# Two GIN layers on one core: all strided copies of layer 2 stored behind the dense stage, and 110 rows of edges summed from natural tiles first

## What is computed

```python
def _gin_conv(x, src, dst, n, W1, b1, gamma, beta, W2, b2):
    agg = jax.ops.segment_sum(x[src], dst, num_segments=n)
    h = x + agg
    h = jax.nn.relu(_batchnorm(h @ W1 + b1, gamma, beta))
    return jax.nn.relu(h @ W2 + b2)

h = jnp.maximum(_layernorm(x, axis=-1), 0.0)
h = _batchnorm(h, g0, b0)
h = jax.nn.relu(_gin_conv(h, src, dst, n, W1a, b1a, g1, bt1, W1b, b1b))
h = _gin_conv(h, src, dst, n, W2a, b2a, g2, bt2, W2b, b2b)
return x + jax.nn.relu(h)
```

## Time and profile before

| | us |
|---|---|
| median of 3 runs (2820.1 to 2820.8) | 2820.61 |
| the profiled execution | 2806.54 |
| its span, from the first to the last instruction | 2804.7 |
| PE busy | 2380.3 (85%) |
| POOL busy | 1846.7 (66%) |
| DVE busy | 1734.9 (62%) |
| ACT busy | 528.8 (19%) |
| DMA, mean rate over the span | 262 GB/s |

### The profile page before, as it was taken

How to read it: one execution, slowest core, us unless ns; L and a number is a source line. 1 busy time by engine, 2 the same in 40 slices (tenths; PEclk the granted TensorE clock), 3 DMA queues, 4 the chain that set the end, 5 groups by cost and what they waited for, 6 DMA issues and landing times.

```text
span 2804.7 us, 30481 instructions
## 1 busy us (share of the span) xinstructions
PE 2380.3 (85%) x10221; PEld 1829.1 (65%) x10221; DVE 1734.9 (62%) x3349; ACT 528.8 (19%) x1542; POOL 1846.7 (66%) x1870
## 2 busy tenths in 40 slices
PE   1466657999999999999998666799999999989879
PEld 1133424788777777777776544588888888776767
DVE  6999995655555555555556577655555555544459
ACT  8963534300000000000007611100000000000038
POOL 2058886777777777777770277777777777777720
PEclk8685766999999999999998899999999999999999
DMA  9387994888888888888874999988888888888868
GB/s 307 144 263 203 300 311 123 254 267 254 254 254 254 254 254 253 254 254 254 253 242 161 338 354 353 301 282 288 284 284 287 284 283 287 259 254 254 253 204 271
DMA packets 309073, 735.46 MB, mean 262 GB/s; under 512 B 41126, under 2 KB 183346, under 8 KB 308910
## 3 DMA queue, kind: packets, MB, share of 16 engines
q0 software_dynamic: 148896, 552.17, 62.7%
q1 hardware_dynamic: 160014, 181.25, 20.0%
HBM read 580.67 MB, written 152.59 MB: 261 GB/s over the span
## 4 chain that ended last, share of the span: by engine, by line
PE 49%; DMA 21%; POOL 13%; SPq 7%; issue 5%; ACT 5%; DVE 1%; DVEq 0%; ACTq 0%; POOLq 0%
PE agg_ps L815 33%; DMA rows<-node_rows,src_all 19%; POOL rows L687 8%; SPq L610 7%; PE mm_ps L940 6%; PE mm_ps L857 5%; POOL rows L672 3%; PE mm_ps L861 2%; POOL raw_more L672 2%; ACT acc L985 2%; ACT lane_code L972 1%; PE agg_ps L769 1%; ACT lane_code L961 1%; DMA raw_more<-node_rows,src_all 1%; DMA node_rows<-acc 1%
## 5 line engine op out<-in xcount | busy, mean ns | idle before, releaser
L687 POOL DMA_INDIRECT rows<-node_rows,src_all x1672 | 1580.4, 945 | 647.6 <-issue 347.9
L815 PE MATMUL agg_ps<-rows,work 128*128 128x256 f32 (+1 forms) x7106 | 1662.4, 387 | 179.7 <-DMA rows<-node_rows,src_all 136.0
L815 PEld LDWEIGHTS agg_ps<-rows,work 128*128 128x128 f32 x7106 | 1311.0, 190 | 502.9 <-DMA rows<-node_rows,src_all 122.9
L1514 DVE SCALAR_TENSOR_TENSOR acc<-agg_ps,in_first,acc 128x256 f32 (+1 forms) x289 | 140.0, 485 | 955.9 <-PE agg_ps L815 880.7
L1016 ACT ACTIVATE bn_root<-bn_var 128x2 f32<-128x2 f32 x3 | 0.6, 204 | 1891.1 <-DVE bn_var L1146 1891.1
L672 POOL DMA_INDIRECT rows<-node_rows,src_all x96 | 137.2, 1429 | 166.2 <-DMA node_rows<-acc 137.2
L1466 DVE TENSOR_TENSOR work<-lane_code,lane_ps 128x1024 f32<-128x1024 f32 (+1 forms) x209 | 231.6, 1108 | 1.1 <-issue 1.1
L940 PE MATMUL mm_ps<-early,work 128*128 128x256 f32 x784 | 176.1, 389 | 20.0 <-ACT work L1095 11.4
L940 PEld LDWEIGHTS mm_ps<-early,work 128*128 128x128 f32 x784 | 141.0, 194 | 55.3 <-issue 23.4
L1475 DVE TENSOR_TENSOR work<-lane_code,lane_ps 128x640 f32<-128x640 f32 x209 | 169.8, 812 | 0.0
L1095 ACT ACTIVATE work<-acc,bn_shift,bn_scale 128x128 f32<-128x128 f32 x392 | 167.3, 485 | 3.3 <-DVE bn_shift L1157 2.8
(11 more groups left out here) (250 smaller groups left out, 1663.7 us busy)
## 6 DMA issues: line engine op xcount, KB each, us to landing
node_rows<-acc SPq DMA_DIRECT2D x113, 260.0 KB, 5.7
rows<-node_rows,src_all POOLq DMA_INDIRECT x1768, 4.3
node_rows<-acc SPq DMA_DIRECT2D x27, 910.0 KB, 4.3
node_rows<-acc SPq DMA_DIRECT2D x57, 390.0 KB, 5.9
node_rows<-acc SPq DMA_DIRECT2D x28, 650.0 KB, 7.7
node_rows<-acc SPq DMA_DIRECT2D x114, 130.0 KB, 4.6
acc<-in_x SPq DMA_DIRECT2D x13, 896.0 KB, 11.0
rows<-in_x SPq DMA_DIRECT2D x13, 896.0 KB, 7.4
```

Of the source, the lines that this page charges most:

```text
L687: pool.indirect_dma_start(tile_rows(k, 0, ROWS_OF[t] * DP), None, tables[layer][0:NPOS if t >= LAST_STRIDED else TABLE, :], bass.IndirectO ...
L815: mm = pe.matmul(bank[:, 0:width], hot[:, unit * P:(unit + 1) * P], tile_rows(k, row, width), start=(start and n == 0), stop=(stop and n = ...
L1514: dve.scalar_tensor_tensor(to, sums, lanes[:, g:g + 1], to, ALU.mult, ALU.add).then_inc(sums_added, 1)
```

## The change

`TWICE` becomes `NR`: all 110 rows are visited twice, so that the natural pass has 220 gathers in place of 160 and the strided pass 660 in place of 720. SP no longer issues copies between the chunks of the dense stage; all 217 follow when the last pieces have been issued. `BESIDE` is gone. Nothing else is edited.

```diff
-TWICE = 80
+TWICE = NR
 ONLY_STRIDED = range(LAST_STRIDED)
 ONLY_NATURAL = range(LAST_STRIDED, T)
 GROUP = 2 * CH
 GROUPS = NB // GROUP
-BESIDE = 8 * P
...
             copies = copies_by_group()
             for c in range(NCH - 1):
                 store_rows(1, c, y_out, (c + 1) * CH)
-                rows_beside = 0
-                while c % 2 + c // 2 and rows_beside < BESIDE:
-                    i, to, of = next(copies)
-                    sp.dma_start(to, of).then_inc(group_stored[i], 16)
-                    rows_beside += of.shape[0] * of.shape[1]
             store_last_rows()
             for i, to, of in copies:
                 sp.dma_start(to, of).then_inc(group_stored[i], 16)
```

## The result

The changed kernel took **2837.9 us** (median of 4 runs, 2837.7 to 2838.5), the kernel before 2820.4 beside it (4 runs, 2819.3 to 2820.8): ratio **1.0065, interval 1.0049 to 1.0081**, 17.5 us slower. The forecast was 2836, +15.6.

A forecast was written before the change was run, and what follows sets the result against it. Layer 2 was taken as bound by GpSimd's 880 gathers at 1.25 us; start -6, row 14 +7, later groups about +2, drain about +11 made +14.6, with tail +1 +15.6, on the median 2820.6: 2836 us, range 2819 to 2846.

The forecast's parts named there:

- the drain: From group 6's landing, VectorE's undone natural rows hold GpSimd at the strided tiles: 37.4 us to gather 234, about +11 us.
- the tail: TensorE's last row past the last gather: starts 2.5 us later, six matmuls fewer, +1 us (0 to 3).
- pauses for later groups: GpSimd's waits for copy groups after group 0 in layer 2's natural pass: about +2 us.
- The start: Layer 2's first gather starts earlier without copies ahead of the last pieces: 6.1 us gained (3.9 to 7.4).
- The copies: All 217 copies follow the dense stage; with pieces and gathers 95.5 MB at 344 GB/s, group 6 in at 1861.
- the bound of 1892: Late bound for group 6's landing, in us, if all seven groups took group 2's 44.0 us.
- Row 14: GpSimd stops at layer 2's row 14 until group 0 is scaled, added and summed: about 7 us lost.
- rival B: TensorE's clock falls at group waits and stays low for 16 rows after group 6: +7 us, 2843; chance 9%.
- Rival C: DMA engines serve gathers first, copies keep 186 GB/s, 40.1 us a group, group 6 about 1869: 2844 us; chance 9%.
- The footing: Increment from the 2806.5 us profiled execution carries over to the runs' median of 2820.6 us, 14.1 above: 2836.

The follow-up runs named there:

- change again: The changed kernel without any edit, run again with more runs beside the kernel before: 2822.6 us against 2806.1, ratio 1.0059 (1.0045 to 1.0073).
- third time: The changed kernel without any edit, run once more for another profile of the stretch after group 6 lands: 2822.1 us.

## Why the prediction was right, and where its terms were off

The direction, the mechanism and the sum against the timed runs held. Part of the closeness is terms that cancelled: in the two later traces group 6 came 2 to 7 us earlier than forecast, and the drain and the tail took 3 to 4 us more. By steps, each trace counted from its own last block (before: 1583.04 us), all in us:

| step | before | forecast | after | change again | third time |
|---|---|---|---|---|---|
| first gather | 9.6 | 3.5 | 2.1 | 2.1 | 2.1 |
| pause at row 14 | 0 | 7 | 12.5 | 8.3 | 8.3 |
| pauses for later groups | 0 | 2 | 9.0 | 2.9 | 0 |
| group 6 in | 208.2 | 278.0 | 290.7 | 270.8 | 275.7 |
| group 6 to gather 234 | | 37.4 | 39.1 | 39.6 | 40.1 |
| pauses in the drain | 0 | 11 | 11.8 | 4.5 | 12.0 |
| last gather | 1108.1 | 1122.7 | 1137.1 | 1119.5 | 1123.0 |
| TensorE's last sum past it | 5.6 | 6.6 | 8.5 | 7.8 | 7.9 |
| sum against before | | +15.6 | +32.0 | +13.7 | +17.2 |

(A pause is counted beyond the usual 0.30 us between two gathers, and above 0.6 us; what the rows leave over, 2 to 3.3 us in each trace of the change, are smaller ones.)

*The start* gained 7.5 us, a little above the upper bound of 7.4. With nothing queued ahead of the last piece the first gather started 2.06 us after the last block was written, as the kernel's own last store suggested (at most 2.1 us); I had moved 1.4 us away from that row for copies that are issued behind the piece, and the runs show no cost of them.

*The copies*, with the pieces and gathers beside them, were 94.84 MB in 291 us (forecast 95.5 in 278). The DMA page of after between 1583 and 1874, as the earlier trace rows:

```profile
q1 hardware_dynamic: 53841, 52.36, 62.1%
q0 software_dynamic: 13543, 42.30, 43.4%
```

The bytes were right, and so was the rate of the earlier trace rows in two of the three traces (346 and 349 GB/s from 1588 to 1791 us); in the first it was 5% lower, and 1873.4 lies between 1861 and the bound of 1892. That one rate makes most of the first trace's excess. Why the DMA engines gave 326 GB/s in that session isn't settled: the queues, their bytes and their share of time are nearly the same. The later sessions ran on chips 4, 0 and 13, and none is on record for the first, so a difference between chips isn't excluded.

*Row 14* stopped as foreseen, by group 0. In the first trace the term was 5.5 us short, because group 0 landed 44.2 us after the last block (forecast 40). In the other two it was 1.3 us short, though group 0 landed at 40.1, because the earlier start brings GpSimd to the row sooner: the gain of one term is the loss of the other.

*The drain* was the deciding term and came within 2 to 3 us: 37.4 forecast from group 6 to gather 234, 39.1 to 40.1 measured. From there 646 gathers took 807.3 us in after (2719.81 - 1912.55), as forecast. Most of the missing part is a small piece of rival B. TensorE in after, timeline: the first rows of the drain, and the last two rows of layer 2.

```profile
1875.98 4.29 PE L809 MATMUL agg_ps<-rows,work 128*128 128x256 f32 x12 [5.69 <-DVE work L1450]
1881.59 1.56 PE L809 MATMUL agg_ps<-rows,work 128*128 128x256 f32 x6 [1.32 <-DVE work L1450]
...
2717.28 1.13 PE L809 MATMUL agg_ps<-rows,work 128*128 128x256 f32 x4 [0.45 <-DMA rows<-node_rows,src_all]
2718.24 1.89 PE L851 MATMUL mm_ps<-early 128*128 128x256 f32 x8
2719.97 1.46 PE L809 MATMUL agg_ps<-rows,work 128*128 128x256 f32 x6
...
2726.45 1.89 PE L809 MATMUL agg_ps<-rows,work 128*128 128x256 f32 x8
```

After 5.69 us of waiting, the twelve matmuls of two rows took 4.29 us instead of twice 1.56, at a granted clock of 0.63 over those 4 us, between the lower level of 1.2 GHz (0.50) and the full 2.4. VectorE's adds stand 3.49 us apart there instead of 2.12 (1876.26 to 1879.75), then 2.12 again. (The bracket there names ScalarE, which was still scaling the group's later blocks; at group 5, at 1833.72, it was doing the same, but TensorE's six matmuls kept their 1.56 us and the adds stood 2.42 and 2.25 apart.) So the clock did fall at a group's wait. This agrees with the rule named under rival B: the Trainium skill, "TensorE: Matmul & The Clock Gate", Part 1, says that the clock falls after idling. But here it was back within one row to three. The trace of the change again has the longest such stretch:

```profile
1859.62 6.66 PE L809 MATMUL agg_ps<-rows,work 128*128 128x256 f32 x15 [4.44 <-DVE work L1450]
```

Fifteen matmuls took 6.66 us in place of 3.90 (at 1.56 for six). There the clock was 0.50 from 1860 to 1864 us and 0.81 from 1864 to 1868, and two of VectorE's steps were longer (3.49 and 2.57). That costs 1.4 to 1.8 us a drain, not the 7 of sixteen rows.

*Rival C* can't be told from the forecast by the groups' spacing: 38.5, 39.3 and 41.1 us in three traces of one kernel, on both sides of the 39.56 and the 40.1 that stood against each other. Its core is true, though. GpSimd kept issuing a gather every 1.25 us beside the copies, and the copies alone were at 25.5 us a group: it was mainly they that were slowed. This agrees with the rule named under rival C: by the Trainium skill, "DMA: Bandwidth & Descriptors", Queues, rings and completion order, an engine takes turns between the queues a whole packet at a time. The gathers took longer to land too, 6.9 us in the median from 1583 to 1874, where it is 4.5 over the whole kernel.

*The tail* was +2.3 to +2.9, at the upper end (0 to 3) of a term taken at +1. TensorE begins the last row 0.16 us after the last gather is issued (2719.97, 2719.81), before 4.2 us ahead of it: 4.4 us later, where the working had 2.5 for the distance between two tiles' issues. Products with the next weights stand directly ahead of it in both kernels (L851, L857), so they don't explain the difference. The other 1.9 us arose one row earlier: TensorE reached those products 5.9 us after the last gather of that row was issued (2718.24, 2712.31), before 4.1 us after it (2685.20, 2681.12). In after it waited 0.45 us for a tile just ahead of them; the rest of the cause stays open. The versions with 100 rows measure the same term by its absence: their TensorE ends 6.0 and 6.3 us after the last gather.

*The footing.* The prediction added its increment to the runs' median although its trace was of a quicker execution, and that was right by the times: +17.5 and +16.5 in two sessions whose absolute times differ by 14 to 15. No row stood behind that step, so as far as the prediction goes the fit to the first session's absolute time was luck: the traces of before and after, to which its terms belong, differ by 31.5 us, twice the forecast sum. In the first session both kernels were slower by about this much. For the changed kernel its trace shows where (group 6 some 15 to 20 us later), and the runs with twelve more copies show that either kernel passes such a lateness on whole. That the kernel before waited for its groups in the timed runs of that session fits this, but no trace of such a run of it exists, so it stays open.

*A reading.* The prediction calls GpSimd's idle time all "issue"; the earlier trace rows puts 347.9 of 647.6 us to it. For the stretch from 1790 us on, which the argument uses, shows no wait above 0.3 us, so nothing hung on it.

## What to carry to other kernels

Before moving transfers out of a stage, see what the stage that receives them has left: here they left a stretch in which no gather wanted the DMA engines and joined one that was full, and GpSimd's seemingly free time in front of them was other work that had to be summed after the same transfers. If only the last pieces are held up, take away just those transfers that stand directly ahead of them. And when a buffer ring meets a late input, price the drain: the consumer's rows still undone at that moment, times its own pace, less what the ring holds.

## What the runs showed of the hardware

- A store of the last piece on empty engines landed so that the first gather started 2.06 us after the last block was written, in three traces of the change; with four copies ahead 9.6.
- SP's 217 copies alone moved 288 GB/s at a DMA share of 0.93, less than the 344 to 346 of the mixture with gathers. SP took 0.82 us for each (178.1 / 217); whether its issuing or the DMA engines set that pace wasn't separated.
- One and the same kernel got 326 GB/s in one session and 346 in another, at the same share of 1.06. The full share told that the engines were occupied, not how fast they moved bytes.
- After a wait of 5.69 us TensorE ran its next twelve matmuls in 4.29 us in place of 3.12, at a mean granted clock of 0.63, and from 1880 us on it was at 1.00 again; after one of 4.44 us in the change again the next fifteen took 6.66 us in place of 3.90.
